# Rows scattered into expert slots without an inverse map, and four batches of attention ahead of the experts

## The reference

```python
xn = _layernorm(x, axis=-1)
x = x + attn(xn, w_qkv, b_qkv, w_out, b_out) + ffn(xn, w12, w3, gate_w)
# attn: 16 heads of 16; windows of 128 rows, one every 64; of the windows' rows, in order, the first 512 of a batch are kept
scores = einsum('bhnqd,bhnkd->bhnqk', qw, kw) / sqrt(16)
ow = einsum('bhnqk,bhnkd->bhnqd', softmax(scores), vw);  o = ow @ w_out + b_out
# ffn: 8 experts, the two with the highest gate scores for each row
topk_scores, topk_idx = top_k(einsum('btd,ed->bte', xn, gate_w), 2);  p = softmax(topk_scores)
expert = (silu(xn @ w1[e].T) * (xn @ w2[e].T)) @ w3[e].T;  y = sum over the two of p * expert
```

## Time and profile before

| | |
|---|---|
| Median of 3 runs | 712.89 us (712.26 to 713.5) |
| Profiled execution | 713.24 us, of which 711.5 us is its span |
| PE busy | 633.2 us (89%) |
| DVE busy | 571.6 us (80%) |
| ACT busy | 513.7 us (72%) |
| POOL busy | 280.4 us (39%) |
| DMA moved | 92.74 MB, 130 GB/s on average |

### The profile page before, as it was taken

How to read it: one execution, slowest core, us unless ns; L and a number is a source line. 1 busy time by engine, 2 the same in 40 slices (tenths; PEclk the granted TensorE clock), 3 DMA queues, 4 the chain that set the end, 5 groups by cost and what they waited for, 6 DMA issues and landing times.

```text
span 711.5 us, 17988 instructions
## 1 busy us (share of the span) xinstructions
PE 633.2 (89%) x5916; PEld 512.0 (72%) x5917; DVE 571.6 (80%) x906; ACT 513.7 (72%) x883; POOL 280.4 (39%) x330
## 2 busy tenths in 40 slices
PE   0786776978999999999999999999889899999995
PEld 0564554754888888888888888888767676666673
DVE  4958899975688888888888888888687979788884
ACT  4554477474687787787777777777667788888885
POOL 3000273031344444444444444444300336666654
PEclk9998788998999999999999999999999999999999
DMA  9895477581111111111111111112168687885840
GB/s 300 268 257 174 128 262 273 146 284 31 49 53 52 59 52 52 59 53 50 59 55 50 57 56 51 56 54 56 45 161 258 174 259 180 271 227 161 215 138 30
DMA packets 66384, 92.74 MB, mean 130 GB/s; under 512 B 6448, under 2 KB 53424, under 8 KB 66320
## 3 DMA queue, kind: packets, MB, share of 16 engines
q1 hardware_dynamic: 57904, 70.56, 33.3%
q0 software_dynamic: 6864, 18.75, 7.9%
q10 hardware_dynamic: 1568, 2.76, 1.2%
HBM read 59.06 MB, written 32.83 MB: 129 GB/s over the span
## 4 chain that ended last, share of the span: by engine, by line
PE 63%; DVE 14%; ACT 10%; issue 8%; DMA 2%; POOL 2%; ACTq 0%; SPq 0%; DVEq 0%; POOLq 0%
PE PS L1300 55%; PE PS L1549 4%; DVE SMALL L964 4%; ACT WORK L781 3%; DVE XN L1122 2%; PE PS L1527 2%; DVE WALL L958 2%; ACT QS L776 1%; DMA XN<-in_x 1%; DVE WORK L1033 1%; DVE WORK L1026 1%; POOL OTS L595 1%; ACT WORK L719 1%; DVE WALL L982 1%; DMA KS<-parts_scratch 1%
## 5 line engine op out<-in xcount | busy, mean ns | idle before, releaser
L367 DVE TENSOR_TENSOR WS<-WALL,WS 128x1024 fp32r<-128x1024 f32 x136 | 166.9, 1227 | 56.0 <-ACT WS L862 41.5
L1300 PE MATMUL PS<-WS,XTS 128*128 128x512 f32 x804 | 203.9, 402 | 0.0
L1300 PEld LDWEIGHTS PS<-WS,XTS 128*128 128x128 f32 x804 | 146.2, 189 | 30.5
L862 ACT ACTIVATE WS<-WALL 128x1024 fp32r x136 | 143.7, 1056 | 9.1 <-issue 0.3
L1300 PE MATMUL PS<-DOWN_HIGH,HTS 128*128 x568 | 108.3, 290 | 5.0 <-DVE DOWN_LOW L958 3.5
L595 POOL TENSOR_TENSOR OTS<-SIDE,XN 128x256 f32<-128x256 f32 x31 | 23.8, 768 | 209.2 <-DVE XN L1122 142.2
L1300 PEld LDWEIGHTS PS<-DOWN_HIGH,HTS 128*128 128x128 f32 x568 | 86.4, 190 | 5.5 <-issue 5.5
L964 DVE TENSOR_REDUCE SMALL<-PS 128x8 f32<-128x1024 f32 x64 | 77.5, 1211 | 12.6 <-PE PS L1300 12.4
L781 ACT ACTIVATE WORK<-PS 128x512 f32<-128x512 f32 x128 | 69.4, 594 | 24.8 <-PE PS L1300 21.4
L658 POOL DMA_INDIRECT ys_scratch<-SIDE,SIDX x36 | 43.8, 1215 | 97.0 <-ACT SIDE L893 97.0
L654 POOL DMA_INDIRECT XS<-xn_scratch,GIDX x72 | 70.4, 978 | 23.6 <-issue 21.6
(11 more groups left out here) (148 smaller groups left out, 1094.8 us busy)
## 6 DMA issues: line engine op xcount, KB each, us to landing
WALL<-in_wexp SPq DMA_DIRECT2D x28, 384.0 KB, 7.1
WALL<-ys_scratch SPq DMA_DIRECT2D x16, 512.0 KB, 7.3
parts_scratch<-WORK SPq DMA_DIRECT2D x32, 240.0 KB, 2.5
QS<-parts_scratch SPq DMA_DIRECT2D x16, 480.0 KB, 4.6
XN<-in_x SPq DMA_DIRECT2D x4, 1024.0 KB, 12.1
xn_scratch<-XN SPq DMA_DIRECT2D x4, 1024.0 KB, 7.2
WALL<-in_x SPq DMA_DIRECT2D x8, 512.0 KB, 5.7
KS<-parts_scratch SPq DMA_DIRECT2D x16, 240.0 KB, 3.9
```

Source lines behind the costliest of these rows:

```text
L367: eng.tensor_tensor(out=WS[:, 1 - k, half, 1], in0=weights, in1=WS[:, 1 - k, half, 0].bitcast(F32), op=ALU.subtract).then_inc(low_ready[ha ...
L862: act.activation(WS[:, 1 - k, half, 0], weights, ACT.Copy).then_inc(high_ready[half], 1)
L1300: return pe.matmul(o, a, b, start=start, stop=stop)
```

## The change

The rows in `XN` get a 257th column. It holds, as an integer, the place to which the row's expert result belongs: the row's number for the best expert, that plus 4096 for the second. POOL scatters each of the 32 tiles twice from SBUF to its slots in `xs_scratch`, and 7 tiles of zeros with dump rows to the slots that stay empty (`pads` finds those on DVE, eight operations of at most 56 columns): 71 indirect DMAs, of 128 rows of 1028 bytes, `SCATTERS` of them behind the divides of windows 0 to 14. The inverse map and all that makes it go, as do the gathers and the store of `xn_scratch`. In the experts SP loads a tile of `xs_scratch` whole, two tiles ahead, behind `keep` of batch 3 and all scatters; POOL copies its last column to `SIDX`.

`EXTRA` becomes 4: batches 0 to 3 go ahead of the experts, with their results kept in `XOUT`, and batches 4 to 7 follow. Batches 5 to 7 add their own experts' rows; the 20 tiles of batches 0 to 4 are spread over the windows of batches 4 to 7 by `LATER_AT`. SP's order in a batch of stage 1 is parts, `rest(b + 1)`, `rows_back(b - 3)`, `load_tokens`. The weights of experts 6 and 7 are loaded in batch 2. The down weights of experts 4 and 5 are split last, since their buffers now hold `XOUT` and `DENS`. Not shown below: the removal of `store_xn`, `tags`, `places`, `make_places`, `part_of_places`, `take_map`, `slot_map` and their waits, and buffers and semaphores.

```diff
@@ -42,23 +42,21 @@
 XS_TILES = SLOT_TILES + 1
 KT = 2 * NT
 DUMP_ROW = 2 * B * L
+PADS = SLOT_TILES * P - 2 * B * L
+PAD_TILES = PADS // P
+ROW = D + 1
 EARLY = 4
 FIRST_EXPERTS = 1
 LATE = 6
-PLACES_POOL = (0, 0, 8, 16)
-PLACES_ACT = 24
-PLACES_EACH = 4
-PLACES_FROM = PLACES_POOL[-1] + PLACES_ACT
 LAST = B - 1
-MAP_UNIT = 2
 EXACT_UP = 4
-DOWN_ORDER = (3, 4, 0, 1, 2, 5, 6, 7)
+DOWN_ORDER = (3, 0, 1, 2, 6, 7, 5, 4)
 DOWN_AT = (0, 1, 4, 6, 8)
 BY_DVE_ALONE = 2
-EXTRA = 2
-OWN = 3
-LATER = {4: 2, 5: 0, 6: 1}
-FIRST_LATER = min(LATER)
+EXTRA = 4
+OWN = EXTRA + 1
+LATER_AT = ((0, 1, 1, 2), (1, 1, 1, 2), (1, 1, 1, 2), (2, 2, 2, 0))
+SCATTERS = (4,) + (5,) * 13 + (2,)
 WU, WD = NC_D * 2 * FH, FC * D
 WE = WU + WD
 EPS = 1e-5
...
@@ -130,7 +127,9 @@
                 return shared(name, shape, dt)
 
         WS = shared("WS", [P, 2, 2, 2, NC_D, FH], F32R)
-        XN = sb("XN", [P, NT, D])
+        XROWS = sb("XN", [P, NT, ROW])
+        XN = XROWS[:, :, 0:D]
+        IDS = XROWS[:].bitcast(I32)[:, :, D:ROW]
         DOWN_LOW = shared_behind(WU, "DOWN_LOW", [P, E * WE - WU], F32R)
         WALL = sb("WALL", [P, E * WE])
         stack = H * SPAN // 2
...
@@ -459,6 +439,7 @@
 
             def rows_back(b):
                 t = slice(b * TB, (b + 1) * TB)
+                sp.wait_ge(rows_out[b], 16)
                 sp.dma_start(XN[:, t, :], rv[:, t, :]).then_inc(rows_in[b], 16)
                 rest(b)
 
@@ -477,45 +458,56 @@
 
             def keep(b):
                 sp.wait_ge(r_free, (b + 1) * NWIN + 1)
-                t = slice(b * TB, (b + 1) * TB)
-                sp.dma_start(rv[:, t, :], XN[:, t, :]).then_inc(rows_out, 16)
+                sp.dma_start(rv[:, b * TB:(b + 1) * TB, :], XOUT[:, b % 2]).then_inc(rows_out[b], 16)
 
             begin(0)
             load_experts(FIRST_EXPERTS, EARLY - 1)
             sp.wait_ge(early_done, 1)
             load_tokens(1)
             load_experts(EARLY - 1, LATE)
-            begin(1)
-            sp.wait_ge(map_done, 1)
-            load_experts(LATE, E)
-            keep(0)
-            load_tokens(2)
-            keep(1)
-            sp.wait_ge(rows_out, 16 * EXTRA)
+            for b in range(1, EXTRA):
+                begin(b)
+                keep(b - 1)
+                load_tokens(b + 1)
+                if b == 2:
+                    sp.wait_ge(temps_done, 1)
+                    sp.wait_ge(pads_out, 16 * PAD_TILES)
+                    load_experts(LATE, E)
+            keep(EXTRA - 1)
+            sp.wait_ge(firsts_out, 16 * NT)
+            sp.wait_ge(seconds_out, 16 * NT)
+            sp.wait_ge(pads_out, 16 * PAD_TILES)
+            xsv = xs_dram.rearrange("(j p) d -> j p d", p=P)
+            for j in range(XS_TILES):
+                if j > 1:
+                    sp.wait_ge(xt_full, j - 1)
+                    sp.wait_ge(ids_taken, j - 1)
+                sp.dma_start(XS[:, j % 2, :], xsv[min(j, SLOT_TILES - 1)]).then_inc(xs_in[j % 2], 16)
             sp.wait_ge(y_stored, 1)
+            rows_back(0)
             sp.dma_start(KS[STK:DEEP, 1], KS[STK:DEEP, 0]).then_inc(hot_back, 16)
 
-            def send_later(n, b):
-                sp.wait_ge(later_ready, (n + 1) * TB)
-                t = slice(b * TB, (b + 1) * TB)
+            def send_later(src):
+                sp.wait_ge(later_ready, (src + 1) * TB)
+                t = slice(src * TB, (src + 1) * TB)
                 sp.dma_start(ov[:, t, :], XR[:, t, :]).then_inc(out_done, 16)
 
             for b in range(EXTRA, LAST):
                 begin(b)
                 rest(b + 1)
+                rows_back(b + 1 - EXTRA)
                 if b < LAST - 1:
                     load_tokens(b + 1)
-                if b + 2 in LATER:
-                    if LATER[b + 2] < EXTRA:
-                        rows_back(LATER[b + 2])
-                    else:
-                        rest(LATER[b + 2])
-                if b > OWN:
-                    send(b - 1)
-                    if b - 1 in LATER:
-                        send_later(b - 1 - FIRST_LATER, LATER[b - 1])
+                if b == EXTRA + 1:
+                    send_later(0)
+                if b == EXTRA + 2:
+                    send_later(1)
+                    send(EXTRA + 1)
+            rest(EXTRA)
+            send_later(2)
             send(LAST - 1)
-            send_later(LAST - 1 - FIRST_LATER, LATER[LAST - 1])
+            send_later(3)
+            send_later(EXTRA)
             for n in range(NWIN):
                 sp.wait_ge(r_free, LAST * NWIN + n + 2)
...
@@ -607,16 +588,16 @@
                 pool.wait_ge(rest_in[b], 48)
                 combine(b * TB + n, BOUT[:], own_ready)
 
-            def later(b, n):
-
-                pool.wait_ge(later_scaled, 2 * ((b - FIRST_LATER) * TB + n + 1))
-                src = LATER[b]
+            def later(i):
+
+                src, n = divmod(i, TB)
+                pool.wait_ge(later_scaled, 2 * (i + 1))
                 pool.wait_ge(rest_in[src], 48)
                 if src < EXTRA:
                     pool.wait_ge(rows_in[src], 16)
                 else:
...
@@ -625,52 +606,60 @@
                 link(pool.tensor_tensor(out=SLOT, in0=SLOT, in1=BASE.unsqueeze(1).to_broadcast([P, NT, E]), op=ALU.add))
                 for k, one_hot in enumerate((OH1, OH2)):
                     link(pool.tensor_tensor(out=PICK, in0=SLOT, in1=one_hot, op=ALU.mult))
-                    add_experts(SLOTF[:, k, :], PICK)
-
-                slots = SLOTF.rearrange("p k t -> p (k t)")
-                link(pool.tensor_scalar(out=TILE, in0=slots, scalar1=1.0 / P, scalar2=-(P - 1) / (2.0 * P),
-                                        op0=ALU.mult, op1=ALU.add))
-                link(pool.tensor_scalar(out=TILE, in0=TILE, scalar1=ROUND, scalar2=None, op0=ALU.add, op1=ALU.bypass))
-                link(pool.tensor_scalar(out=TILE, in0=TILE, scalar1=-ROUND, scalar2=None, op0=ALU.add, op1=ALU.bypass))
-                pool.sem_inc(tiles_ready, 1)
-                link(pool.tensor_scalar(out=TMPS, in0=TILE, scalar1=-float(P), scalar2=None, op0=ALU.mult, op1=ALU.bypass))
-                link(pool.tensor_tensor(out=IN_TILE, in0=slots, in1=TMPS, op=ALU.add))
-                link(pool.tensor_scalar(out=LESS, in0=IN_TILE, scalar1=-1.0, scalar2=None, op0=ALU.mult, op1=ALU.bypass))
-                pool.wait_ge(xn_out, 64)
-                pool.wait_ge(tok_full, NT // 2)
-                pool.wait_ge(xt_out[LAST], 16)
-                pool.wait_ge(scored, B)
-                pool.sem_inc(tiles_ready, 1)
-
+                    add_experts(SLOTF[:, k * NT:(k + 1) * NT], PICK)
+
+                link(pool.tensor_copy(SLOTS[:, 0:KT], SLOTF))
+                pool.wait_ge(pads_ready, 1)
+                link(pool.tensor_copy(SLOTS[:, KT:], PADF))
+                pool.wait_ge(xn_ready, NT)
+
+            sent = Count()
+
+            def send(at, rows, done):
+                pool.indirect_dma_start(xs_dram, bass.IndirectOffsetOnAxis(SLOTS[:, at:at + 1], 0),
+                                        rows, None).then_inc(done, 16)
+
+            def send_rows(n):
+
+                for i in range(sent.now(), sent.add(n)):
+                    if i < NT:
+                        send(i, XROWS[:, i, :], firsts_out)
+                    elif i < NT + PAD_TILES:
+                        send(i + NT, PAD_ROWS[:, i - NT, :], pads_out)
+                    else:
+                        t = i - NT - PAD_TILES
+                        if t == 0:
...
+                            pool.wait_ge(firsts_out, 16 * NT)
+                            link(pool.iota(IDS, [[P, NT], [1, 1]], base=B * L, channel_multiplier=1))
+                        send(NT + t, XROWS[:, t, :], seconds_out)
+
+            link(pool.iota(IDS, [[P, NT], [1, 1]], base=0, channel_multiplier=1))
+            pool.wait_ge(xt_out[LAST], 16)
+            pool.wait_ge(scored, B)
+            link(pool.memset(PADROWS, 0.0))
+            link(pool.iota(PAD_IDS, [[P, PAD_TILES], [1, 1]], base=DUMP_ROW, channel_multiplier=1))
             divide(0)
             find_slots()
-            for w in range(1, 3):
-                divide(w)
-                make_places(w)
-            for w in range(3, 6):
-                divide(w)
-
-            def gather(j):
-                pool.indirect_dma_start(XS[:, j % 2, :], None, xn_dram,
-                                        bass.IndirectOffsetOnAxis(GIDX[:, j:j + 1], 0)).then_inc(xs_in[j % 2], 16)
+            for w, n in enumerate(SCATTERS):
+                if w:
+                    divide(w)
+                send_rows(n)
+            divide(EXTRA * NWIN - 1)
 
             def scatter(j):
-                pool.indirect_dma_start(ys_dram, bass.IndirectOffsetOnAxis(SIDX[:, j:j + 1], 0),
+                pool.indirect_dma_start(ys_dram, bass.IndirectOffsetOnAxis(SIDX[:, j:j + 1].bitcast(U32), 0),
                                         YS[j % 2], None).then_inc(y_out[j % 2], 16)
 
-            pool.wait_ge(map_done, 1)
```

(48 more changed lines are left out.)

173 lines of the change are left out of this document (41 added, 132 removed).

## The result

The changed kernel takes 779.6 us (median of 4 runs, 775.88 to 786.06) against 712.76 beside it (712.26 to 713.5): 1.0945 times the time, with an interval of 1.089 to 1.1. It is slower, as forecast, but by 66.8 us where 18.4 had been worked out, and far above the range of 708 to 740. The profiled execution took 775.88 us with a span of 774.1, 62.6 more than before.

The account below looks back on a forecast made before the run. DVE was taken to bound batch 0, PE the experts, and PE with little slack elsewhere the later batches. Terms from -15.4 to +7.5 summed to +18.4 on 713.24: 731.6, as median 731.3 us; range 708 to 740.

Parts of the forecast that it names:

- DVE's relief: Batches ahead of the experts, mainly batch 0: tags, places and map go from DVE; 15.4 us gained in all.
- The fourth rival: Batch 0: DVE's relief worth 5 us less, since ACT and PE have own delays; 736, within the forecast's 0.62.
- Scatters on POOL: Windows 0 to 14: five issues and a divide overrun the short windows; 1.5 us lost, bounds 0.7 to 11.
- the second rival: Batches 1 to 3: POOL is the bound, issues taking 1.33 us; 9.5 us more, 741; chance 0.04.
- Weights against parts: Batch 1: twelve weight transfers in SP's queue delay the parts of batch 2; 3 us lost, between 0 and 9.
- Entry to the experts: First expert rows load behind the kept rows of batch 3, so PE starts late; 3.9 us, bounds 3 and 5.
- SP's queue: Batches 4 to 6: rows read back delay the token load and ACT's scaling; 4.8, 6.5 and 7.5 us lost.
- The first rival: SP's queue in batches 4 to 6: transfers don't hold each other up; 20.8 us less, 710.5; chance 0.2.
- PE's clock after a stop: Batches 4 to 6: PE may run at a lower clock after three waits; 2 us lost, between 0 and 6.
- Tail: Last batch: POOL has two late tiles and one own in each of three windows; 4.6 us, bounds 2 and 6.

Follow-up runs that it names:

- f1_rows_earlier: Changed kernel, scatters as they are, SP issuing the expert rows behind the experts one batch earlier and behind the token load: 765.93 us, ratio 1.0731.
- the fourth of the last kernels: Changed kernel, SP's order mended, 67 scatters dealt 3, 3, 6, 6 per batch, expert weights spread behind token loads, 3072 bytes for descriptors: 753.73 us.
- the experts with the dummy: Kernel before, with one more 128-row scatter behind each of the experts' 71 tiles: cost 15.1 us, a tile taking 5.08 us instead of 4.85.
- the third kernel: Changed kernel, SP's order mended, 67 scatters dealt 3, 3, 6, 6 per batch, expert weights spread behind token loads, descriptor memory unchanged: 748.47 us.

## Why the prediction was wrong, step by step

I set the four batches against batches 0 to 3 of before: 141.3 us there (74.8 from the first reciprocal at 78.53 to the last of batch 1 at 153.36, and 66.4 for batches 2 and 3). Of the 15.4 us of relief 0.2 belong to batch 4, so the forecast for them was 141.3 - 15.2 + 1.5 + 3 = 130.6; measured 168.9, a miss of 38.3.

- **DVE's relief, 15.4: right.** Without scatters, and less what the weights cost (below), the four batches took 133.5 - 5.95 = 127.6 us, 13.7 less than before, where 15.2 were worked out. Batch 0 took 42.95 instead of 41.9; its first window, the one with `pads`, took 17.49 instead of 16.05. The fourth rival had put the relief 5 us lower, it is 1.5.
- **Scatters on POOL, 1.5 (0.7 to 11): wrong, the step that failed.** They cost 168.9 - 133.5 = 35.4 us (41.7 in f1_rows_earlier, which is the same program up to there). The time of an issue was right: 0.96 us in the median of 71, plus 0.30, so the second rival (issues of 1.33) falls as it was put. What failed is the step that counts nothing but an overrun of POOL's own time. I read the price of an indirect DMA in the experts, two in 4.85 us with POOL idle for the rest of it, and used it for five in a row in 7 to 9 us. The harm falls on PE, whose matmuls come apart and whose signals reach ACT and DVE late, and my upper bound, made of POOL's durations alone, couldn't see it. POOL's stops were at nothing in the sum too: three of them, 13.6 us of POOL's time; PE's waits for divides came to 8.2 us against 4.6 without scatters. The 33.9 us are seven eighths of the miss here; 2.95 for the weights and 1.5 for DVE are the rest.
- **Weights against parts, 3 (0 to 9): low.** 38.65 - 32.7 = 5.95 us without scatters, within the bounds; beside the scatters nothing of it can be told.
- **Entry to the experts, 3.9: right.** 377.5 - 373.8 = 3.7; PE waited 4.43 us for the first rows.
- **SP's queue: right in place and size.** The waits after show, in batch 4, PE's for the tokens (first fence), in batch 5 PE's for ACT and ACT's scaling for the rows (second), in batch 6 ACT's again (third):

```profile
PE PS L1248 <- DMA WORK<-xt_scratch: 4.4, 1, 4.4
```

```profile
PE PS L1248 <- ACT WORK L770: 7.2, 1, 7.2
...
ACT WALL L785 <- DMA WALL<-ys_scratch: 7.0, 1, 7.0
```

```profile
ACT WALL L785 <- DMA WALL<-ys_scratch: 8.2, 1, 8.2
```

  The forecast had 4.8, 6.5 and 7.5. Moving these transfers alone took 6.9 and 8.4 us out of batches 5 and 6. The first rival (transfers that don't hold each other up) falls with these waits. Batches 4 to 6 grew by 9.0, 7.7 and 10.5 us against 34.0 (593.60 to 627.57), 34.0 and 27.5 (661.55 to 689.07) before, 27.2 in all, where the three waits and the clock had been put at 20.8.
- **PE's clock after a stop, 2 (0 to 6): low.** The granted clock is 0.92, 0.92 and 0.87 in the three batches; in f1_rows_earlier, where two of the waits are gone, it is 1.00 again in two of them. With 2.9 us for late KS parts in batch 4, which I hadn't had, this is where the 6.4 us above lie; I can't part them further.
- **Tail, 4.6: right.** From the last batch's first reciprocal 26.3 us instead of 22.4, 3.8 more. The divides around the three windows stand 22.5 us apart (743.25 and 765.74), where 22.0 had been worked out, with POOL without a pause between them.

In sum 38.3 of the span's 44.2 us of miss (62.6 against 18.4) lie ahead of the experts, the rest behind them; the median of the runs lies 3.7 above the profiled one. The forecast had the direction from the queue behind the experts; the larger cause wasn't in its sum. The chance of 0.04 for anything above 740 came from a rival whose mechanism was POOL's slowness, not that of its neighbours.

**What stays open.** It is shown that beside rows of indirect DMAs PE's ready matmuls come apart and PE's signals reach ACT and DVE late, that it is bound to the issue and not to rows or bytes, that 20 plain DMAs from POOL, at 3.5 us, don't do it, and that it came with five in each window of the kernel before and not with four. Why PE is held up isn't shown. Whether gathers do it as scatters do wasn't tried.

One rival stands untested: the recording itself. Of the semaphores' rises that instructions cause, 112 of 559 are missing in the trace of the changed kernel's four batches, 109 of 552 in the fourth of the last kernels, 78 of 551 with three scatters in a window, where two starts are late by 1 us, and 195 of 1071 in the experts with the dummy. Where no start is late behind PE, nearly all are there (550 of 550 without scatters, 549 of 550 in the third kernel, all with plain DMAs). Every execution on record carries a span and a clock from the profiler. So no run tells how much of the loss would be there without it.

## What to carry to other kernels

The price of an operation is that of its density: before moving indirect DMAs from a stage where they are thin to one where they would stand in a row, put a few dummies there in the old kernel; here 20 of them cost 15 us in one run, ten times what had been put for all 71. A moved operation is to be priced by what it does to the other engines, so the wait list's "issue" and "remote" entries belong to its cost. And where several transfers share one queue, what lies behind the new one can be worked out well from landing times: the three waits came out within 0.7 us, though the batches grew by 6.4 us more than the waits and the clock had been put at.

## What the runs showed of the hardware

- 71 scatters with nothing beside them took 100.3 us, 1.41 each: 0.96, 0.30 between, and a stop of 2.2 to 2.9 us whenever the memory for descriptors came round. Beside the batches the stops took 1.7 to 7.0 us. With 16 rows a scatter 20 went without a stop, at 0.84 us each.
- Beside rows of scatters the semaphore that PE raises with a product rose up to 7.6 us after the product's modelled end, as at 110.65 above; ACT, waiting for it, started at once.
- An issue isn't held up by DVE's casts in the batches. The scatter at 136.01 took 0.96 us, as any, with this beside it:

```profile
136.01 0.96 POOL L619 DMA_INDIRECT xs_scratch<-XN,SLOTS  x1 [0.30 <-issue]
```

```profile
136.25 0.33 DVE L1012 CAST WORK<-WORK 128x320 bf16<-128x320 f32 x1
```

  The rule of the Trainium skill (SBUF — State Buffer, section "Who interferes with whom") that such a cast locks POOL out of its descriptors while it runs doesn't show in this trace: ten of the scatters ran beside such casts, at 0.96 to 1.08 us, and the casts took 0.33 us as they do alone.
